# Attention block on one core: value projection by seven block products of 256 columns, position tiles in another order

## The chip, the cores and the metric

One core of a Trainium2 chip runs the whole program. The metric is the device time in microseconds (us), the median of several runs. TensorE (PE; its weight loads are listed as PEld) multiplies, VectorE (DVE), ScalarE (ACT) and GpSimd (POOL) do the element-wise work, SyncE (SP) issues most DMAs.

## The reference, cut to what matters

```python
residual = hidden_states                 # (16, 512, 32, 32), f32
h = group_norm(hidden_states, gamma, beta)
q, k, v = conv1x1(h, wq, bq), conv1x1(h, wk, bk), conv1x1(h, wv, bv)
attn = softmax(einsum('bci,bcj->bij', qf, kf) * C ** -0.5, axis=2)
out = einsum('bcj,bij->bci', vf, attn)
return residual + conv1x1(out, wo, bo)
```

There are 16 images of C = 512 channels and N = 1024 positions.

## The kernel before, in words

**Precision.** A factor of a product is split into a high part (`*_hi`, rounded to the fp32r format) and a low part (`*_lo`, the rest). One `product` (L346 to L349) is three matmuls of 128x128 weights with 512 moving columns: high by high (L347), high by low (L348), low by high (L349). ACT makes the high parts by a copy, DVE the low parts by a subtraction, so that each factor passes ACT and then DVE before PE may use it.

**Weights.** Wk and Wq are multiplied into one matrix before the loop, and so are Wv and Wo. Both joint matrices, split, are kept in DRAM (`kept_t`, `kept_v`), and take turns in the tile `w_split`.

**The stages of PE in an image**, in this order:

1. T (`make_t`): joint Wq/Wk matrix by h. It uses seven block products in place of eight (a Strassen-like scheme), with sums of blocks of h, named S1 to S4, beside the plain blocks A11, A12, A22. 84 matmuls.
2. S (`make_scores`): scores of 1024 x 1024, the same scheme, 168 matmuls. DVE adds up the blocks (`add_s`) and takes the running maximum (`maximum`).
3. V (`make_v`): values, 8 position tiles j of 128 positions x 512 columns, each 4 products of plain blocks (8 block products): 96 matmuls.
4. O0 (`outputs_0`): outputs for the first 512 queries. Outer loop over the 8 position tiles j, inner loop over 4 channel tiles c. 96 matmuls.
5. O1 (`outputs_1`): the other 512 queries. Here c is the outer loop: the first channel tile asks for all 8 position tiles within 24 matmuls. 96 matmuls.

**The softmax** goes beside V, O0 and O1, in two halves of 512 queries. POOL reduces the maximum over partitions (L322, after `maximum`), DVE subtracts it from the scores (`centre`, two tiles a time), ACT takes the exponentials (`exponentials`, two tiles a time), ACT rounds a tile (`high_p`), DVE makes its low part (`low_p`). Then DVE adds the exponentials up (`add_up`), POOL sums over partitions (L333), DVE inverts the sum (`inverse`), and multiplies the outputs by it (`output`). ACT adds a bias, POOL issues an accumulating DMA into `out`.

**The next image** is prepared in O0 and O1: its x is loaded into `room` (`full_in`), ACT normalises it in four pieces (`normalise`), DVE forms S1 to S4 (`sum_h`, four operations), ACT rounds the seven blocks (`high_h`), DVE makes the low parts (`low_h`).

**What sets the order.** There is no scheduler: each engine has one written list of operations, and semaphores hold an operation until what it needs is there. An operation that waits holds everything behind it on its engine. In O1 the wait is this one:

```python
for c in range(KC):
    for j in range(NJ):
        if c == 0:
            pe.wait_ge(p_split, count(b, 16, NJ + j + 1))
```

The first image runs apart (it makes the weights), images 2 to 15 run in a loop, and the last has no next image to prepare (`more` is false).

Of the kernel before, what the change touches and what calls it, by code (L numbers as in the profile page):

```python
# [13 lines left out]
P = 128  # L14
# [22 lines left out]
H_ORDER = (A22, S1, A12, S3, S2, A11, S4)  # L37
H_AT = {x: n + 1 for n, x in enumerate(H_ORDER)}

# [11 lines left out]
G_AT = {PRODUCT_OF[x]: n + 1 for n, x in enumerate(G_ORDER)}  # L51

# [4 lines left out]
def attention_program(nc, x, gamma, beta, wq, bq, wk, wv, bv, wo, bo, out):  # L57
# [17 lines left out]
    TW, VW = 7 * 2 * QUARTER, 3 * 2 * C  # L75
    kept_t = nc.dram_tensor("kept_t", [P, 2, TW], F32).ap()
    kept_v = nc.dram_tensor("kept_v", [P, 2, VW], F32).ap()

    with ExitStack() as ctx:
# [9 lines left out]
        wv_hi, wv_lo = (w_split[:, n, 0:VW].rearrange("p (b k n) -> p b k n", b=3, k=2) for n in range(2))  # L89
# [18 lines left out]
        var_g, rstd, minus_half, primer = sb("var_g", [KC]), sb("rstd", [KC]), sb("minus_half", [KC]), sb("primer", [2])  # L108
        h_scale, h_shift, mean_scaled = sb("h_scale", [KC]), sb("h_shift", [KC]), sb("mean_scaled", [KC])
# [30 lines left out]
        wov_step = scores[:, 14:16, :]  # L140
# [16 lines left out]

        wt_from = {1: b11, 2: b21, 3: b22, 4: neg_d4, 5: d1, 6: d2, 7: d3}
# [3 lines left out]
        v_ring = (6, 7, 4, 5)  # L162
# [11 lines left out]
        full_in = [sem("full_in0"), sem("full_in1")]  # L174
# [29 lines left out]
        o_scaled, o_done = sem("o_scaled"), sem("o_done")  # L204
# [14 lines left out]
        def _(sp):  # L219
# [13 lines left out]
            def image(b, more, first=False):  # L233
# [17 lines left out]
                if first:  # L251

                    sp.wait_ge(t_split, 14)
# [3 lines left out]
                    sp.wait_ge(wvs_split, 3)  # L257
                    for n in range(6):
                        piece(n)
                else:  # L260
                    sp.wait_ge(t_summed, count(b, 14, 14))
                    sp.dma_start(w_split[:, :, 0:VW].bitcast(F32), kept_v).then_inc(wvs_in, 16)
                if more:
# [3 lines left out]
                    if first:  # L267
                        sp.dma_start(kept_v, w_split[:, :, 0:VW].bitcast(F32)).then_inc(kept_v_out, 16)

                    sp.wait_ge(bn_set, count(b, PIECES, 2 * PIECES))  # L270
                    sp.wait_ge(s_added, count(b, 12, 12))
                    for s in range(2):
                        sp.dma_start(full[:, 2 * s:2 * s + 2, :],
                                     x_d[b + 1][:, 2 * s:2 * s + 2, :]).then_inc(full_in[s], 16)
                    sp.wait_ge(v_summed, count(b, 8, 8))
# [69 lines left out]
        def _(pe):  # L345
# [54 lines left out]
            def make_t(b, first=False):  # L400
# [3 lines left out]
                for r in range(2):  # L404
# [3 lines left out]
                    for p in T_ORDER:  # L408
                        if r == 0:
                            pe.wait_ge(h_split, count(b, 7, H_AT[OF_H[p]]))  # L410
# [68 lines left out]

            def make_v(b, first=False):  # L480
                if first:
                    pe.wait_ge(wvs_split, 3)
                else:
                    pe.wait_ge(wvs_in, count(b, 16, 0))
                for j in range(NJ):
                    if j < 2:
                        pe.wait_ge(s_added, count(b, 12, ADD_AT["C21", j]))
                    elif j == 2:
                        pe.wait_ge(c12_copied, count(b, 4, 4))
                    elif j == 3:  # L490
                        pe.wait_ge(s_added, count(b, 12, ADD_AT["C11", 2]))
                    else:
                        pe.wait_ge(v_split, count(b, 8, j - 4 + 1))

                    terms = ((A11, 0), (A12, 1)) if j < KC else ((S1, 0), (A22, 2))
                    for a, w in terms:
                        for k in range(2):
                            mm = product(bank[v_ring[j % 4]][:], h_hi[:, a, k, cols(j % KC)], h_lo[:, a, k, cols(j % KC)],
                                         wv_hi[:, w, k, :], wv_lo[:, w, k, :], w == 0 and k == 0, w > 0 and k == 1)
                    mm.then_inc(v_summed, 1)  # L500

            def outputs_0(b):
                for j in range(NJ):
                    pe.wait_ge(v_split, count(b, 8, j + 1))
                    pe.wait_ge(p_split, count(b, 16, j + 1))
                    for c in range(KC):
                        if j == 0:
                            if c == 0:
                                pe.wait_ge(c12_copied, count(b, 4, 3))
                            else:  # L510
                                pe.wait_ge(s_added, count(b, 12, 12))
                        mm = product(o_bank(c)[:], v_hi[:, j, cols(c)], v_lo[:, j, cols(c)],
                                     p_hi[:, j, :], p_lo[:, j, :], j == 0, j == NJ - 1)
                        if j == NJ - 1:
                            mm.then_inc(o_summed, 1)
                    if j < NJ - 1:
                        mm.then_inc(p_used, 1)

            def outputs_1(b):
                for c in range(KC):  # L520
                    for j in range(NJ):
                        if c == 0:
                            pe.wait_ge(p_split, count(b, 16, NJ + j + 1))
                        mm = product(o_bank(KC + c)[:], v_hi[:, j, cols(c)], v_lo[:, j, cols(c)],
                                     p_hi[:, j, :], p_lo[:, j, :], j == 0, j == NJ - 1)
# [17 lines left out]
        def _(act):  # L543
# [14 lines left out]
            def high_h(b, n, first=False):  # L558
                a = H_ORDER[n]
# [49 lines left out]
            def high_wv(n):  # L609

                act.wait_ge(t_summed, 14)
                act.wait_ge(kept_t_out, 16)
                if n == 2:
                    act.wait_ge(wdv_set, 1)
                else:
                    act.wait_ge(wov_copied, KC)
                nc.scalar.copy(wv_hi[:, n, :, :], wov_step if n == 2 else wov[n]).then_inc(wvs_high, 1)
# [17 lines left out]
            def high_v(b, j):  # L635
                act.wait_ge(v_summed, count(b, 8, j + 1))
                nc.scalar.copy(v_hi[:, j, :], bank[v_ring[j % 4]][:]).then_inc(v_high, 1)  # L637

            def exponentials(b, half, g):
                j = half * NJ + 2 * g  # L640
                act.wait_ge(centred, count(b, 8, half * 4 + g + 1))
# [3 lines left out]
            def high_p(b, half, j):  # L645
                act.wait_ge(exp_set, count(b, 8, half * 4 + j // 2 + 1))
                if half == 1 and j < NJ - 1:
                    act.wait_ge(p_used, count(b, NJ - 1, j + 1))
# [11 lines left out]
            def image(b, more, first=False):  # L660
# [39 lines left out]
                for pair in range(2):  # L700
                    for n, p in enumerate((1, 6, 5)):
                        for q in (2 * pair, 2 * pair + 1):
# [4 lines left out]
                            nc.scalar.copy(snap_s(q, n), bank[alpha_s[q % 2]][:]).then_inc(s_snapped, 1)  # L707
                    for q in (2 * pair, 2 * pair + 1):
# [6 lines left out]
                high_v(b, 0)  # L715
                high_v(b, 1)
                for g in range(4):
                    high_v(b, 2 + g)
                    exponentials(b, 0, g)
                    high_p(b, 0, 2 * g)  # L720
                    high_p(b, 0, 2 * g + 1)
                high_v(b, 6)
                high_v(b, 7)
                for g in range(4):
# [4 lines left out]
                for j in range(3):  # L729
                    high_p(b, 1, j)  # L730
                for j in range(3, NJ):
                    high_p(b, 1, j)
# [435 lines left out]
```

## Time and profile before

| | us |
|---|---|
| median of 3 runs | 2022.17 (2019.12 to 2023.99) |
| profiled execution, its own time | 2020.75 |
| its span, first to last instruction | 2019.0 |
| mean granted TensorE clock | 0.999 |

The page counts PE busy for 99% of the span, DVE and the weight loads for 81%, ACT for 47%, POOL for 16%. Busy shares are averages over stages; in a timeline row the second number is the busy time of the row's instructions, which on DVE and ACT overlap by some 0.1 us where they follow each other, so that the step from one start to the next is the price of one.

### The profile page before, as it was taken

Reading aid. Unit: us, or ns where it says so; the run is one execution under the profiler, and the core shown is the slowest. Engines: PE = TensorE matmul, PEld = TensorE weight load, DVE = VectorE, ACT = ScalarE, POOL = GpSimd, SP = SyncE. Lnnn points to the kernel's source line nnn. Section 1 sums busy time; section 2 is a strip of 40 time slices with the busy share of each in tenths; the row PEclk is TensorE's granted clock in tenths of the full one; section 3 lists DMA queues with packets and bytes.
Section 4 is the critical chain, followed back from the end, with each engine's and each line's share of the span. In section 5 each row is a group of like instructions: output and inputs, shape, how many; then the busy total and the mean of one; then the engine's idle time right before and its main releaser. Section 6 shows DMA issues by size and latency. Waiting matters only on the chain.

```text
span 2019.0 us, 26696 instructions
## 1 busy us (share of the span) xinstructions
PE 1998.6 (99%) x8772; PEld 1645.1 (81%) x8772; DVE 1625.5 (81%) x2120; ACT 956.7 (47%) x1429; POOL 329.8 (16%) x238
## 2 busy tenths in 40 slices
PE   8999999999999999999999999999999999999998
PEld 6888888888888888888888888888888888888887
DVE  8897787978879688796977969788797887969866
ACT  6464442635435463454634536354363543546442
POOL 2021120201202022020121202112020120201202
PEclk9999999999999999999999999999999999999999
DMA  6335252353324435143351523524234342433402
GB/s 240 131 157 147 97 133 105 128 140 156 75 112 140 120 156 118 69 149 111 156 145 69 152 87 150 145 116 113 114 124 136 156 81 105 145 114 156 103 2 42
DMA packets 57033, 247.03 MB, mean 122 GB/s; under 512 B 7728, under 2 KB 7728, under 8 KB 50352
## 3 DMA queue, kind: packets, MB, share of 16 engines
q1 hardware_dynamic: 36464, 213.14, 27.8%
q0 software_dynamic: 18432, 33.56, 11.0%
q10 hardware_dynamic: 2112, 0.01, 0.1%
q8 instruction: 14, 0.23, 0.0%
q14 instruction: 11, 0.09, 0.0%
HBM read 206.32 MB, written 73.92 MB: 139 GB/s over the span
## 4 chain that ended last, share of the span: by engine, by line
PE 89%; DMA 5%; DVE 2%; ACT 1%; issue 1%; POOL 0%; SPq 0%; DVEq 0%; POOLq 0%; ACTq 0%
PE psum L347 30%; PE psum L348 30%; PE psum L349 30%; DMA out<-scores 5%; ACT scores L657 1%; DVE scores L895 0%; DVE wide L1023 0%; DMA scores<-in_wk 0%; DVE bn L756 0%; DVE h_lo L825 0%; POOL out L339 0%; DVE w_split L874 0%; ACT h_hi L564 0%; DVE scores L1029 0%; DVE scores L1015 0%
## 5 line engine op out<-in xcount | busy, mean ns | idle before, releaser
L347 PE MATMUL psum<-big_hi 128*128 128x512 f32 x1056 | 411.5, 390 | 2.8 <-POOL big_lo L297 2.8
L349 PE MATMUL psum<-big_hi,big_lo 128*128 128x512 f32 x1056 | 411.5, 390 | 0.0
L348 PE MATMUL psum<-big_lo,big_hi 128*128 128x512 f32 x1056 | 411.5, 390 | 0.0
L347 PE MATMUL psum<-big_hi,h_hi 128*128 128x512 f32 x896 | 350.1, 391 | 0.8
L349 PE MATMUL psum<-big_hi,h_lo 128*128 128x512 f32 x896 | 348.7, 389 | 0.0
L348 PE MATMUL psum<-big_lo,h_hi 128*128 128x512 f32 x896 | 348.7, 389 | 0.0
L982 DVE TENSOR_TENSOR scores<-psum,room 128x512 f32<-128x512 f32 x192 | 130.8, 689 | 187.3 <-ACT room L707 137.3
L707 ACT COPY room<-psum 128x512 f32<-128x512 f32 x192 | 113.1, 589 | 273.3 <-PE psum L349 273.3
L347 PEld LDWEIGHTS psum<-big_hi 128*128 128x128 f32 x1056 | 198.7, 188 | 44.8 <-DVE big_lo L850 3.0
L349 PEld LDWEIGHTS psum<-big_hi,big_lo 128*128 128x128 f32 x1056 | 198.6, 188 | 41.4
L348 PEld LDWEIGHTS psum<-big_lo,big_hi 128*128 128x128 f32 x1056 | 198.6, 188 | 41.1
L322 POOL PARTITION_ALL_REDUCE wide<-red x32 | 56.9, 1830 | 893.0 <-DVE red L991 893.0
L347 PEld LDWEIGHTS psum<-big_hi,h_hi 128*128 128x128 f32 x896 | 168.2, 188 | 41.1 <-issue 6.6
L347 PE MATMUL psum<-w_split,h_hi 128*128 128x512 f32 x512 | 199.2, 389 | 0.0
L348 PE MATMUL psum<-w_split,h_hi 128*128 128x512 f32 x512 | 199.2, 389 | 0.0
L349 PE MATMUL psum<-w_split,h_lo 128*128 128x512 f32 x512 | 199.2, 389 | 0.0
L349 PEld LDWEIGHTS psum<-big_hi,h_lo 128*128 128x128 f32 x896 | 168.2, 188 | 35.1
L348 PEld LDWEIGHTS psum<-big_lo,h_hi 128*128 128x128 f32 x896 | 168.2, 188 | 34.4
L651 ACT CAST big_hi<-scores 128x512 fp32r<-128x512 f32 x256 | 147.8, 619 | 77.0 <-PE psum L349 74.9
L347 PE MATMUL psum<-h_hi,w_split 128*128 128x512 f32 x448 | 176.1, 393 | 8.1 <-DVE h_lo L825 4.5
L637 ACT CAST big_hi<-psum 128x512 fp32r<-128x512 f32 x128 | 75.4, 589 | 223.4 <-PE psum L349 223.4
L333 POOL PARTITION_ALL_REDUCE wide<-red x32 | 117.7, 3680 | 368.8 <-DVE red L1019 354.9
(117 smaller groups left out, 3274.3 us busy)
## 6 DMA issues: line engine op xcount, KB each, us to landing
w_split<-kept_t SPq DMA_DIRECT2D x15, 3584.0 KB, 11.1
w_split<-kept_v SPq DMA_DIRECT2D x15, 3072.0 KB, 10.6
out<-scores POOLq DMA_DIRECT2D x128, 256.0 KB, 7.4
room<-in_x SPq DMA_DIRECT2D x30, 1024.0 KB, 5.9
room<-in_x SPq DMA_DIRECT2D x60, 256.0 KB, 3.5
red<-in_x SPq DMA_DIRECT2D x30, 256.0 KB, 3.3
wide<-in_x SPq DMA_DIRECT2D x30, 256.0 KB, 7.1
kept_t<-w_split SPq DMA_DIRECT2D x1, 3584.0 KB, 10.9
```

The source lines that it names most:

```text
L322: nc.gpsimd.partition_all_reduce(wide[:, half, :], red[:, half, :], P, MAX_ALL).then_inc(max_all, 1)
L333: nc.gpsimd.partition_all_reduce(wide[:, half, :], red[:, half, :], P, ADD_ALL).then_inc(sum_all, 1)
L347: nc.tensor.matmul(o, a_hi, b_hi, start=start, stop=False, skip_group_check=True)
L348: nc.tensor.matmul(o, a_hi, b_lo, start=False, stop=False, skip_group_check=True)
L349: return nc.tensor.matmul(o, a_lo, b_hi, start=False, stop=stop, skip_group_check=True)
L637: nc.scalar.copy(v_hi[:, j, :], bank[v_ring[j % 4]][:]).then_inc(v_high, 1)
L651: nc.scalar.copy(p_hi[:, j, :], scores[:, half * NJ + j, :]).then_inc(p_high, 1)
L657: nc.scalar.activation(scaled(n), scaled(n), ACT.Identity, bias=out_bias[:, c:c + 1]).then_inc(o_done, 1)
L707: nc.scalar.copy(snap_s(q, n), bank[alpha_s[q % 2]][:]).then_inc(s_snapped, 1)
L982: nc.vector.tensor_tensor(scores[:, o, :], bank[at][:], snap_s(q, n), ALU.add).then_inc(s_added, 1)
```

## The change

It has four parts.

- **V**: 28 products with 256 columns in place of 32 with 512: seven block products p in the order 7, 1, 6, 5, 3, 4, 2, each for the four position quarters q in turn. Each is 2 x 3 matmuls: 168 of 256 columns in place of 96 of 512. ACT copies three partial sums for two pairs of quarters out of PSUM (`snap_v`, 6 operations), DVE adds PSUM to them (`add_v`, 6), and ACT and DVE split the four blocks of each pair (`high_v`, `low_v`, 8 each as before). The joint matrix is kept in seven blocks: `kept_v` grows from 3072 to 3584 KB, and the first image makes seven splits of 512 elements for three of 1024, with four differences of blocks ahead.
- **Order of the position tiles** in O0, O1 and the softmax: 4, 5, 6, 7, 0, 1, 2, 3.
- **The next image**: `room` holds the partial sums of V, so its load comes in four pieces, three of them behind `low_v`. The rounding order of h is A22, A12, A11, S1, S3, S2, S4. DVE does `low_h` of the first three, and the first two `sum_h`, between the seventh and the eighth `low_p` of the second half; the other two `sum_h` come behind it. Before, all four `sum_h` stood ahead of the first `low_p`, and one `low_h` stood ahead of the eighth.
- **The inverse** of the sums, `[128, 512]` with equal partitions: a transpose, a reciprocal of 16 columns and a transpose back.

```diff
-H_ORDER = (A22, S1, A12, S3, S2, A11, S4)
+H_ORDER = (A22, A12, A11, S1, S3, S2, S4)
+V_ORDER = tuple((p, q) for p in (7, 1, 6, 5, 3, 4, 2) for q in range(4))
+J_ORDER = (4, 5, 6, 7, 0, 1, 2, 3)
+G_PAIRS = (2, 3, 0, 1)
...
+            def v_product(q, p):
+                at = (alpha_v if p in (1, 6, 5, 3) else gamma_v)[q // 2] + q % 2
+                for k in range(2):
+                    mm = product(bank[at][:, 0:QUARTER], h_hi[:, OF_H[p], k, cols(q)], h_lo[:, OF_H[p], k, cols(q)],
+                                 wt_hi[:, p - 1, k, :], wt_lo[:, p - 1, k, :],
+                                 k == 0 and p in (7, 1, 2), k == 1 and p in (3, 4, 2))
+                mm.then_inc(v_summed, 1)
...
-                for j in range(NJ):
-                    pe.wait_ge(v_split, count(b, 8, j + 1))
-                    pe.wait_ge(p_split, count(b, 16, j + 1))
+                for n, j in enumerate(J_ORDER):
+                    if n == 0:
+                        pe.wait_ge(v_split, count(b, 8, max(VL_AT["C12", 1], VL_AT["C21", 0], VL_AT["C22", 0])))
...
+                    pe.wait_ge(p_split, count(b, 16, n + 1))
...
-                for g in range(4):
-                    if more:
-                        act.wait_ge(full_in[g // 2], count(b, 16, 16))
-                        normalise(b + 1, g)
-                    exponentials(b, 1, g)
...
+                for n in range(4):
+                    if more and n:
+                        next_full(4 - n)
+                    exponentials(b, 1, n)
+                for n in range(NJ):
+                    high_p(b, 1, n)
+                    if more and n == 2:
+                        next_full(0)
+                    if more and 3 <= n < 6:
...
+                        high_h(b + 1, n - 3)
...
+            def add_v(b, x, r):
+                o = v_snap(v_sums[x], r)
+                dve.wait_ge(v_snapped, count(b, 6, 2 * v_sums[x] + r + 1))
+                dve.wait_ge(v_summed, count(b, 28, V_AT[{"C22": 5, "C21": 4, "C11": 2}[x], 2 * r + 1]))
+                nc.vector.tensor_tensor(o, v_pair(gamma_v[r]), o, ALU.add).then_inc(v_added, 1)
...
-                nc.vector.reciprocal(wide[:, half, :], wide[:, half, :]).then_inc(inv_set, 1)
+                nc.vector.transpose(red[:, half, :], wide[:, half, :]).then_inc(turn_step, 1)
+                nc.vector.reciprocal(column[:], red[:, half, :].rearrange("p (n s) -> p n s", s=BLOCK)[:, :, 0]
+                                     ).then_inc(turn_step, 1)
+                nc.vector.transpose(wide[:, half, :].rearrange("p (n s) -> p n s", s=BLOCK),
+                                    column[:].unsqueeze(2).to_broadcast([P, HALF // BLOCK, BLOCK])).then_inc(inv_set, 1)
...
                 add_up(b, 0)
+                for j in range(4):
+                    low_p(b, 1, j)
+                for n in range(4, NJ - 1):
+                    low_p(b, 1, n)
                 if more:
+                    for n in range(3):
+                        low_h(b + 1, n)
 
                     dve.wait_ge(sum_step, count(b, SUM_STEPS, 3))
-                    for n in range(4):
-                        sum_h(b + 1, n)
-                for j in range(NJ - 1):
-                    low_p(b, 1, j)
+                    sum_h(b + 1, 0)
+                    sum_h(b + 1, 1)
+                low_p(b, 1, NJ - 1)
                 if more:
-                    low_h(b + 1, 0)
-                low_p(b, 1, NJ - 1)
+                    sum_h(b + 1, 2)
+                    sum_h(b + 1, 3)
                 add_up(b, 1)
```

**The order of DVE in O0 and O1, before.** Of an image in the loop. Lines L1015 to L1019 are `add_up`, L810 to L818 `sum_h`, L1002 is `low_p`, L825 `low_h`.

```order
L1019 TENSOR_TENSOR red<-scores 128x512
L810 TENSOR_TENSOR scores<-room 128x1024
L812 TENSOR_TENSOR scores<-room 128x1024
L814 REGISTER_ALU
L815 TENSOR_TENSOR scores<-scores,room 128x1024
L817 REGISTER_ALU
L818 TENSOR_TENSOR scores<-room,scores 128x1024
...
L1002 TENSOR_TENSOR big_lo<-scores,big_hi 128x512
L822 ISA
L825 TENSOR_TENSOR h_lo<-room,h_hi 128x1024
L1002 TENSOR_TENSOR big_lo<-scores,big_hi 128x512
L1015 TENSOR_TENSOR scores<-scores 128x2048
```

**The same place after the change.** L1110 ends `add_up` of the first half, L1082 is `low_p` (seven stand in the gap, the seventh just ahead of L901), L904 is `low_h`, L889 to L897 are `sum_h`, L1106 begins `add_up` of the second half.

```order
L1110 TENSOR_TENSOR red<-scores 128x512
...
L901 ISA
L904 TENSOR_TENSOR h_lo<-room,h_hi 128x1024
L901 REGISTER_ALU
L904 TENSOR_TENSOR h_lo<-room,h_hi 128x1024
L901 REGISTER_ALU
L904 TENSOR_TENSOR h_lo<-room,h_hi 128x1024
L889 TENSOR_TENSOR scores<-room 128x1024
L891 TENSOR_TENSOR scores<-room 128x1024
L1082 TENSOR_TENSOR big_lo<-scores,big_hi 128x512
L893 REGISTER_ALU
L894 TENSOR_TENSOR scores<-scores,room 128x1024
```

Between the seventh and the eighth `low_p` there stood one operation of 1024 elements, and there stand five now.

**The order of ACT after the change**, from the first exponentials of the second half on. L698 is `exponentials`, L599 `normalise`, L708 `high_p`, L608 `high_h`.

```order
L599 ACTIVATE room<-room,h_shift,h_scale 128x1024
L705 REGISTER_ALU
L708 CAST big_hi<-scores 128x512
L814 REGISTER_ALU
L605 ISA
L608 CAST h_hi<-room 128x1024
L705 REGISTER_ALU
L708 CAST big_hi<-scores 128x512
L608 CAST h_hi<-room 128x1024
...
L608 CAST h_hi<-room 128x1024
L708 CAST big_hi<-scores 128x512 x2
```

The last `normalise` moved from ahead of the last exponentials to behind the third `high_p`; the three `high_h` stand behind the fourth, fifth and sixth `high_p`.

## Rows read from the trace of the kernel before

**Rows 1.** The page: busy time, share of the span, instructions of each engine
```profile
PE 1998.6 (99%) x8772; PEld 1645.1 (81%) x8772; DVE 1625.5 (81%) x2120; ACT 956.7 (47%) x1429; POOL 329.8 (16%) x238
```

**Rows 2.** Waits: who waited <- for whom: us in total, times, longest
```profile
PE psum L347 <- DVE h_lo L825: 4.5, 3, 1.6
...
PE psum L347 <- DVE scores L895: 2.8, 5, 0.8
...
PEld psum L347 <- DVE scores L895: 8.4, 12, 1.2
```

**Rows 3.** Windows: stretch, busy us (x) of PE, PEld, DVE, ACT, POOL, PEclk, DMA
```profile
900.10:1000.10 100.00, 100.00 (x442) 82.48 (x441) 77.76 (x109) 49.75 (x77) 12.65 (x9) 1.00 0.42 144
```

**Rows 4.** Timeline of PE, first matmuls of three stages: start us, us, instruction
```profile
714.88 0.39 PE L347 MATMUL psum<-w_split,h_hi 128*128 128x512 f32 x1
...
736.64 0.39 PE L347 MATMUL psum<-big_hi 128*128 128x512 f32 x1
...
780.16 0.39 PE L347 MATMUL psum<-h_hi,w_split 128*128 128x512 f32 x1
```

**Rows 5.** Source line L381: duration ns min/median/max, first and last start
```profile
L381 PEld LDWEIGHTS psum<-ident,scores x16: 139/140/225, 18.6 to 20.3; 128*128 128x128 f32 x16
```

**Rows 6.** Timeline of PE around the longest early wait
```profile
23.42 0.47 PE L347 MATMUL psum<-big_hi 128*128 128x512 f32 x1 [2.78 <-POOL big_lo L297]
```

**Rows 7.** Windows (columns as in rows 3), after that wait
```profile
23.80:27.10 3.30, 3.30 (x10) 2.56 (x9) 3.23 (x5) 1.30 (x2) 3.19 (x3) 0.50 0.02 5
```

**Rows 8.** Timeline of DVE, one image from 719 to 766 us
```profile
721.75 2.97 DVE L996 TENSOR_TENSOR scores<-scores,wide 128x1024 f32<-128x1024 f32 x2
...
738.07 4.62 DVE L996 TENSOR_TENSOR scores<-scores,wide 128x1024 f32<-128x1024 f32 x4
...
742.61 2.28 DVE L1015 TENSOR_TENSOR scores<-scores 128x2048 f32<-128x2048 f32 x1
...
746.19 0.69 DVE L1019 TENSOR_TENSOR red<-scores 128x512 f32<-128x512 f32 x1
...
746.92 1.23 DVE L810 TENSOR_TENSOR scores<-room 128x1024 f32<-128x1024 f32 x1
...
748.06 3.26 DVE L812 TENSOR_TENSOR scores<-room 128x1024 f32<-128x1024 f32 x1
...
753.63 4.29 DVE L1002 TENSOR_TENSOR big_lo<-scores,big_hi 128x512 fp32r<-128x512 f32 x7
...
757.85 1.22 DVE L825 TENSOR_TENSOR h_lo<-room,h_hi 128x1024 fp32r<-128x1024 f32 x1
...
759.32 0.69 DVE L1002 TENSOR_TENSOR big_lo<-scores,big_hi 128x512 fp32r<-128x512 f32 x1 [0.25 <-ACT big_hi L651]
...
764.24 3.35 DVE L1023 RECIPROCAL wide<-wide 128x512 f32<-128x512 f32 x1
```

**Rows 9.** Timeline of ACT, the same image
```profile
739.32 1.06 ACT L642 ACTIVATE scores<-scores 128x1024 f32<-128x1024 f32 x1 [0.75 <-DVE scores L996]
...
741.42 1.04 ACT L642 ACTIVATE scores<-scores 128x1024 f32<-128x1024 f32 x1
...
746.53 2.17 ACT L651 CAST big_hi<-scores 128x512 fp32r<-128x512 f32 x4
...
748.60 1.05 ACT L564 CAST h_hi<-room 128x1024 fp32r<-128x1024 f32 x1
...
759.19 1.05 ACT L564 CAST h_hi<-scores 128x1024 fp32r<-128x1024 f32 x1
...
760.13 1.05 ACT L564 CAST h_hi<-room 128x1024 fp32r<-128x1024 f32 x1
```

**Rows 10.** Timeline of POOL, the same image
```profile
719.69 3.56 POOL L322 PARTITION_ALL_REDUCE wide<-red  x2 [54.78 <-DVE red L991]
...
747.09 4.16 POOL L333 PARTITION_ALL_REDUCE wide<-red  x1 [7.56 <-DVE red L1019]
```

**Rows 11.** The page: groups of instructions | busy us, mean ns of one | idle before
```profile
L982 DVE TENSOR_TENSOR scores<-psum,room 128x512 f32<-128x512 f32 x192 | 130.8, 689 | 187.3 <-ACT room L707 137.3
```

More of the change, by code:

```diff
@@ L251, in image @@
                 if first:
-                    sp.wait_ge(t_split, 14)
+                    sp.wait_ge(wvs_split, 7)
+                    for n in range(6):
+                        piece(n)
                     for c in range(KC):
@@ L707, in image @@
                             nc.scalar.copy(snap_s(q, n), bank[alpha_s[q % 2]][:]).then_inc(s_snapped, 1)
+                            if first and pair == 0 and n < 2:
+                                high_wv(3 + 2 * n + q)
                     for q in (2 * pair, 2 * pair + 1):
@@ L729, in image @@
[L729 to L732, printed above, removed]
-                    if more:
-                        act.wait_ge(v_summed, count(b, 8, 8))
-                        high_h(b + 1, j - 3)
+                snap_v(b, 0, 0)
+                snap_v(b, 0, 1)
+                snap_v(b, 1, 0)
+                snap_v(b, 1, 1)
+                exponentials(b, 0, 0)
+                snap_v(b, 2, 0)
+                exponentials(b, 0, 1)
@@ new lines, in image @@
+                snap_v(b, 2, 1)
+                high_v(b, "C22", 0)
+                high_v(b, "C12", 0)
+                exponentials(b, 0, 2)
+                high_v(b, "C12", 1)
+                high_p(b, 0, 0)
+                high_p(b, 0, 1)
+                high_v(b, "C22", 1)
+                high_v(b, "C21", 0)
+                exponentials(b, 0, 3)
+                high_p(b, 0, 2)
+                high_v(b, "C21", 1)
+                high_p(b, 0, 3)
+                high_v(b, "C11", 0)
@@ new lines, in image, with next_full @@
+                high_p(b, 0, 4)
+                high_v(b, "C11", 1)
+                for n in range(5, NJ):
+                    high_p(b, 0, n)
+                def next_full(k):
+                    act.wait_ge(full_in[k], count(b, 16, 16))
+                    normalise(b + 1, k)
+                for n in range(4):
[7 more added lines that the diff above has]
+                    if more and 3 <= n < 6:
+                        act.wait_ge(v_summed, count(b, 28, 28))
+                        high_h(b + 1, n - 3)
@@ L737, in image @@
                 if more:
-                    high_h(b + 1, 5)
-                    high_h(b + 1, 6)
+                    for n in range(3, 7):
+                        high_h(b + 1, n)
                 if first:
@@ L1131, in image @@
                 if more:
-                    for n in range(1, 7):
+                    for n in range(3, 7):
                         low_h(b + 1, n)
```

233 lines of the change are left out of this document (140 added, 93 removed).

## The prediction

> **What bounds the kernel now.** I read the page first: PE is busy 1998.6 of 2019.0 us [rows 1]. The list of waits says that PE waits for almost nothing: 4.5, 2.8 and (its weight loads) 8.4 us in the whole run [rows 2]. Then the windows: in 100 us in the middle 441 weight loads, one to a matmul, so a matmul of 512 columns takes 100 / 441 = 0.2268 us [rows 3]. 540 of them make 122.4 us an image. The kernel is bound by the number of matmul columns, and a saved matmul is a saved 0.227 us, as long as the other engines still deliver in time. So the second reading is the timeline of one image on DVE, ACT and POOL, where the delivery is seen. Its V stage begins at 714.88, O0 at 736.64, and the next image's T stage at 780.16 [rows 4]. I call 714.88 "V" and count from there: T begins at V+65.3.
>
> **V on PE.** Removed: 96 matmuls of 512 columns, 21.8 us. Added: 168 of 256 columns. No row shows 256 columns. Half of 0.2268 is 0.113; the transposes of 128 columns, each with its own weight load, start their 16 loads from 18.6 to 20.3 us [rows 5], 0.113 apart, so a pair of load and matmul can follow the other about as fast. A load's own duration is longer for the usual operands: busy 82.48 us for 441 in [rows 3], 0.187 each, which is the upper bound, if loads can't overlap. I take 0.120, near the two lower rows: 168 x 0.120 = 20.2 us, 1.6 less an image, 25.6 in all. Bounds: 19.0 and 31.4 us. The Trainium skill (TensorE: Matmul & The Clock Gate, Back-to-back issue gap) lists 262 cycles for 256 columns and 518 for 512, at 2.4 GHz 109 and 216 ns; the row has 227 for the latter. By its figure V would take 18.3 us and save 3.4 us an image.
>
> **What comes in beside it.** DVE gets six `add_v`, like L982: mean 689 ns [rows 11], but in a row seven subtractions of the size take 757.85 - 753.63 = 4.22, 0.603 each [rows 8]. 3.6 us. The two reciprocals cost 3.35 each [rows 8]; two transposes and a short reciprocal I put at 1.7 (two passes like a subtraction and some waits; between 1.4 and 3.35), so DVE's sum is unchanged, but 3.6 us of it come early, in V, and 3.3 us are saved late, behind the point that matters. ACT gets six copies, in V, where it has room. The larger weight load, the four pieces of x, the softmax tiles in another order: nothing, since the load has the whole S stage (38 us) and x is wanted only at V+31. The first image's eight extra short DVE operations lie in its S stage: 0, at most 2 us.
>
> **The moved operations: the chain.** All steps in us after V.
>
> 1. POOL's two reductions of the maximum begin at 719.69 and take 3.56 [rows 10]; the first is ready at 6.6. The first two `centre` were held by them and ended at 721.75 + 2.97 [rows 8]: 9.8. Nothing of this moves.
> 2. DVE then does, up to the first `centre` of the second half: 2 `centre` of 1.135 (4 took 742.61 - 738.07 = 4.54 [rows 8]), 6 `add_v`, 8 `low_v`, 8 `low_p` at 0.603, and the three tiny ones of `affine`, 0.5: 16.0, so 25.8. Walking the two lists of ACT and DVE side by side I find 1.0 of waiting. So that `centre` starts at 26.8 and ends at 28.0. Before it started at 23.2. The other three and `add_up` (742.61 to 746.92 [rows 8], 4.3) keep DVE until 35.6.
> 3. ACT now has no break until the seventh `high_p`: exponentials and `normalise` in pairs of 2.10 (741.42 - 739.32), three of them and one exponentials of 0.97; then `high_p` of 0.52 (4 in 2.07) and `high_h` of 0.94 (760.13 - 759.19) [rows 9]. 28.1 + 6.3 + 1.0 + 3 x 0.52 + 1.13 + 4 x 0.52 + 3 x 0.94 = 43.0. (The first `high_p` ends at 36.0, so from here on DVE waits for ACT. PE releases the seventh tile's place at 20.2 + 7 x 2.72 = 39.3, so that isn't the bound.)
> 4. DVE: `low_p` of the seventh tile, 43.1 to 43.7. Then three `low_h` and two `sum_h` of 1.14 (748.06 - 746.92 [rows 8]): 49.4. Handovers between engines add some 0.3. The eighth `low_p` runs from 49.7 to 50.4. The reduction on POOL that held L812 for 3.26 in place of 1.22 [rows 8, 10] now begins at V+36, where DVE waits for ACT anyway.
> 5. PE: O1 begins at 20.2 + 21.8 = 42.0. The first channel tile takes 3 matmuls, 0.68, a position tile, and asks for the eighth at 46.7. It gets it at 50.4. **PE waits about 3.6 us in every image that has a next one.** Before, the eighth `low_p` ended at 760.0 [rows 8], with PE asking at 758.4 + 4.8 = 763.2: 3.2 us to spare.
>
> So T begins at 65.3 - 1.6 + 3.6 = V+67.3. Since the chain runs from POOL's reduction and not from PE, a faster V doesn't help: the wait grows by as much.
>
> **The clock.** At 23.42 PE had waited 2.78 us [rows 6]. Behind it the granted clock was 0.50, the level of 1.2 GHz, with 10 matmuls touching 3.3 us, where 16 do at 0.227 [rows 7, 3]: 1.4 lost. The new wait is longer than that one. One case doesn't say that it happens each time; I take 10 of 15 images.
>
> **Sum** against the profiled execution's 2020.75 (1.4 below the median): -25.6 for V, +15 x 3.6 = 54 for the wait, +14 for the clock, +2 for the first image: 2065.
>
> **Rivals.**
>
> - **Delivery holds, PE stays the bound.** Then the time is 2020.75 - 25.6 = 1995. (With the 109 ns that the Trainium skill's page TensorE: Matmul & The Clock Gate lists it would be 2020.75 - 54 = 1966, an estimate.) For it: all my steps are sums of rows of another order. Against it: even if ACT and DVE had the seventh tile at once when PE frees its place (39.3), the eighth `low_p` would end at 39.5 + 0.5 + 0.7 + 5.7 + 0.7 = 47.1, 0.4 late: 2001. The turning point is a wait of 1.7 us (25.6 / 15). Chance 0.14.
> - **The chain holds, the clock doesn't fall**: 2050; or it falls each time: 2072. Both are within the forecast's own range.
> - **A later wait comes on top.** The outputs' first half is now scaled later against T (V+58 to 61, T at 67.3), its accumulating DMAs land about 3 us later against the T stage, and DVE's first sum of T waits for them. I find 1 us to spare. If it fails by one or two: 2080 to 2095. Chance 0.09.
> - **Weight loads pace V**: 0.187 x 168 = 31.4 us, 9.6 more an image: 2020.75 + 154 = 2175. Against it stand the loads 0.113 apart [rows 5]. Chance 0.03.
> - **Both effects cancel**: a wait between 1.5 and 2.0 and no fall of the clock, which needs the chain 1.6 us shorter than I find: 2018 to 2025. Chance 0.03.
>
> **How the numbers follow.** A measurement of this kernel can tell 0.2%, 4 us, from no change. The forecast (wait 2.4 to 4.5 us, clock from never to always) has 0.71 and spans 2031 to 2086. Steps 2 and 3 carry its width: without any waiting in step 2 the chain is 1 us shorter, 15 in all. I widen the range to 2025 to 2095, which takes in the later wait and makes 0.8. Faster 0.14, same 0.03, slower 0.83.
>
> **What would show it.** Right: PE's list of waits led by the line of `low_p` (L1082), about 15 times, 3.6 us each, 50 us or more in all; its stretches behind them at clock 0.50; V stages of 20.2 us; O0 free of waits. Wrong: no such wait (then DVE's list was faster than my steps), the wait in another place (`h_lo` or `scores` for T), a V stage of 30 us, or the waits there and no fall of the clock.

## The result, and the profile after

| | before | after |
|---|---|---|
| median of 4 runs, us | 2021.0 (2019.12 to 2023.99) | 2061.35 (2060.27 to 2061.74) |
| profiled execution, its own time | 2020.75 | 2061.74 |
| mean granted TensorE clock | 0.999 | 0.988 |

The ratio is 1.0197, 95% interval 1.018 to 1.0215: the change costs 40 us. The forecast was 2065, in a range of 2025 to 2095.

The page, against [rows 1]: PE is busy for 7 us less, and its share fell from 99% to 97%, since the span is longer.

```profile
PE 1991.7 (97%) x9924; PEld 1694.4 (82%) x9924; DVE 1636.6 (79%) x2287; ACT 999.8 (49%) x1529; POOL 329.3 (16%) x238
```

The values, in the view of groups by form. This is one of three such groups, L382 and L383 are alike.

```profile
L381 PE MATMUL psum<-w_split,h_hi 128*128 128x256 f32 x896 | 253.6, 283 | 0.1
```

The list of waits of PE, against the first two of [rows 2], and of its weight loads, against the third:

```profile
PE psum L381 <- DVE big_lo L1082: 50.5, 15, 3.4
...
PE psum L381 <- DVE h_lo L904: 5.9, 4, 1.8
```

```profile
PEld psum L381 <- DVE big_lo L1082: 56.9, 15, 3.8
...
PEld psum L381 <- DVE scores L974: 0.3, 1, 0.3
```

One wait is new, on L1082, `low_p`: 15 times, once for each image that has a next one. What PE waited for in T is nearly gone: `scores` (L895 before, L974 now) took 8.4 us of the weight loads before, and 0.3 now.

The timeline of PE in one image shows the starts of V, O0 and T, as [rows 4] did, and the matmuls on both sides of the wait:

```profile
856.01 0.28 PE L381 MATMUL psum<-w_split,h_hi 128*128 128x256 f32 x1
...
876.17 0.40 PE L381 MATMUL psum<-big_hi 128*128 128x512 f32 x1
...
902.49 0.39 PE L383 MATMUL psum<-big_hi,big_lo 128*128 128x512 f32 x1
...
906.24 0.67 PE L381 MATMUL psum<-big_hi 128*128 128x512 f32 x1 [3.36 <-DVE big_lo L1082]
...
924.96 0.39 PE L381 MATMUL psum<-h_hi,w_split 128*128 128x512 f32 x1
```

V takes 876.17 - 856.01 = 20.16 us, 168 matmuls of 0.120. O1 starts 96 x 0.2268 = 21.8 later, at 897.9, and asks for the eighth tile 21 matmuls on, at 902.7. The step from 902.49 to 906.24 is 3.75, of which 0.23 is the matmul itself: PE lost 3.52. T begins at V+68.95; before it was V+65.3.

The windows view of the stretch behind the wait (columns as in [rows 3]):

```profile
906.40:909.80 3.40, 3.40 (x9) 2.63 (x10) 3.37 (x3) 2.35 (x3) 0.00 (x0) 0.50 0.00 0
```

The granted clock is 0.50, the level of 1.2 GHz: 9 matmuls touch 3.4 us. It fell so behind the wait in 13 of the 15 images.

The chain on DVE in the same image, to be read against [rows 8]. L1075 is `centre`, L1089 `add_v`, L1082 `low_p`, L904 `low_h`, L889 and L891 the first two `sum_h`, L1117 to L1122 the inverse:

```profile
862.65 4.34 DVE L1075 TENSOR_TENSOR scores<-scores,wide 128x1024 f32<-128x1024 f32 x3 [2.05 <-POOL wide L356]
...
866.91 0.69 DVE L1089 TENSOR_TENSOR room<-psum,room 128x512 f32<-128x512 f32 x1
...
883.01 4.63 DVE L1075 TENSOR_TENSOR scores<-scores,wide 128x1024 f32<-128x1024 f32 x4
...
899.21 0.69 DVE L1082 TENSOR_TENSOR big_lo<-scores,big_hi 128x512 fp32r<-128x512 f32 x1 [0.78 <-ACT big_hi L708]
...
899.82 3.49 DVE L904 TENSOR_TENSOR h_lo<-room,h_hi 128x1024 fp32r<-128x1024 f32 x3
...
903.23 1.22 DVE L889 TENSOR_TENSOR scores<-room 128x1024 f32<-128x1024 f32 x1
...
904.36 1.22 DVE L891 TENSOR_TENSOR scores<-room 128x1024 f32<-128x1024 f32 x1
...
905.50 0.69 DVE L1082 TENSOR_TENSOR big_lo<-scores,big_hi 128x512 fp32r<-128x512 f32 x1
...
912.68 0.70 DVE L1117 STREAM_TRANSPOSE red<-wide 128x512 f32<-128x512 f32 x1
...
913.42 0.25 DVE L1119 RECIPROCAL column<-red 128x16 f32<-128x16 f32 x1
...
913.71 0.71 DVE L1122 STREAM_TRANSPOSE wide<-column 128x512 f32<-128x512 f32 x1
```

And ACT, against [rows 9]: L698 is `exponentials`, L708 `high_p`. The last row is the seventh and eighth tile.

```profile
884.26 1.07 ACT L698 ACTIVATE scores<-scores 128x1024 f32<-128x1024 f32 x1 [4.26 <-DVE scores L1075]
...
891.48 1.64 ACT L708 CAST big_hi<-scores 128x512 fp32r<-128x512 f32 x3
...
898.57 1.13 ACT L708 CAST big_hi<-scores 128x512 fp32r<-128x512 f32 x2
```

Counted from V = 856.02, the first `centre` of the second half starts at 27.0, the seventh tile is rounded from 42.55 on, its low part starts at 43.2, three `low_h` and two `sum_h` run from 43.8 to 49.5, and the eighth low part starts at 49.5.

**Where the 41 us of the profiled execution came from**, by stage, each stage counted from its first matmul to that of the next one:

| stage | before | after | sum of the differences |
|---|---|---|---|
| V, 16 | 21.76 | 20.15, the first 20.54 | -25 |
| O0 and O1, 15 | 43.52 | 48.80 (13 with a falling clock), 47.20 (2) | +76 |
| T, 15 | 19.7 in the mean | 19.04, one 19.42 | -9 |
| S, 16 | 38.21 | 38.08 | -2 |
| first image's T | 24.5 | 26.5 | +2 |

The last line is not the change's: the other kernels below had 24.5 to 24.9 there. In this execution a stretch at the lower clock, from 39.4 to 42.8 us, lay inside that T, which began at 35.8; in the kernel before it lay ahead of T, at 23.8.

### The profile page after: what moved, and what is told of

Read it like the earlier page. It is cut to its first block, busy times and chain, and to the rows that moved or that the text cites. A ratio compares the mean times of both kernels' runs of the same rounds, so it can differ in the third digit from the quotient of the medians.

```text
span 2060.0 us, 29828 instructions
## 1 busy us (share of the span) xinstructions
PE 1991.7 (97%) x9924; PEld 1694.4 (82%) x9924; DVE 1636.6 (79%) x2287; ACT 999.8 (49%) x1529; POOL 329.3 (16%) x238
## 4 chain that ended last, share of the span: by engine, by line
PE 70%; DVE 10%; ACT 8%; issue 7%; DVEq 0%; ACTq 0%; POOL 0%; POOLq 0%
PE psum L381 24%; PE psum L382 23%; PE psum L383 23%; DVE h_lo L904 3%; ACT big_hi L708 2%; DVE big_lo L1082 2%; ACT room L599 2%; DVE big_lo L1098 2%; ACT scores L698 2%; ACT h_hi L608 2%; DVE scores L1075 1%; DVE scores L889 1%; DVE room L1089 1%; DVE red L1070 0%; DVE mean_scaled L880 0%
## 5 line engine op out<-in xcount | busy, mean ns | idle before, releaser
L381 PE MATMUL psum<-big_hi 128*128 128x512 f32 x1056 | 421.5, 399 | 53.6 <-DVE big_lo L1082 50.5
L382 PE MATMUL psum<-big_lo,big_hi 128*128 128x512 f32 x1056 | 419.2, 397 | 0.0
L383 PE MATMUL psum<-big_hi,big_lo 128*128 128x512 f32 x1056 | 418.9, 397 | 0.0
L381 PE MATMUL psum<-big_hi,h_hi 128*128 128x512 f32 x896 | 348.7, 389 | 0.0
L382 PE MATMUL psum<-big_lo,h_hi 128*128 128x512 f32 x896 | 348.6, 389 | 0.0
L383 PE MATMUL psum<-big_hi,h_lo 128*128 128x512 f32 x896 | 348.5, 389 | 0.0
L381 PEld LDWEIGHTS psum<-big_hi 128*128 128x128 f32 x1056 | 203.3, 192 | 102.7 <-DVE big_lo L1082 56.9
L381 PE MATMUL psum<-w_split,h_hi 128*128 128x256 f32 x896 | 253.6, 283 | 0.1
L382 PE MATMUL psum<-w_split,h_hi 128*128 128x256 f32 x896 | 253.6, 283 | 0.0
L383 PE MATMUL psum<-w_split,h_lo 128*128 128x256 f32 x896 | 253.6, 283 | 0.0
L383 PEld LDWEIGHTS psum<-big_hi,big_lo 128*128 128x128 f32 x1056 | 203.1, 192 | 43.5
L382 PEld LDWEIGHTS psum<-big_lo,big_hi 128*128 128x128 f32 x1056 | 203.4, 193 | 41.9
L1082 DVE TENSOR_TENSOR big_lo<-scores,big_hi 128x512 fp32r<-128x512 f32 x256 | 198.7, 813 | 24.9 <-ACT big_hi L708 24.9
L356 POOL PARTITION_ALL_REDUCE wide<-red x32 | 56.9, 1827 | 884.5 <-DVE red L1070 884.5
L381 PEld LDWEIGHTS psum<-big_hi,h_hi 128*128 128x128 f32 x896 | 168.2, 188 | 35.3 <-issue 0.5
L383 PEld LDWEIGHTS psum<-big_hi,h_lo 128*128 128x128 f32 x896 | 168.2, 188 | 34.9
L382 PEld LDWEIGHTS psum<-big_lo,h_hi 128*128 128x128 f32 x896 | 168.2, 188 | 34.8
L1075 DVE TENSOR_TENSOR scores<-scores,wide 128x1024 f32<-128x1024 f32 x128 | 162.9, 1324 | 32.7 <-POOL wide L356 32.7
L381 PE MATMUL psum<-h_hi,w_split 128*128 128x512 f32 x448 | 175.5, 392 | 5.9 <-DVE h_lo L904 5.9
L367 POOL PARTITION_ALL_REDUCE wide<-red x32 | 104.1, 3252 | 478.5 <-DVE red L1110 469.5
```

The source lines that it names most:

```text
L356: nc.gpsimd.partition_all_reduce(wide[:, half, :], red[:, half, :], P, MAX_ALL).then_inc(max_all, 1)
L367: nc.gpsimd.partition_all_reduce(wide[:, half, :], red[:, half, :], P, ADD_ALL).then_inc(sum_all, 1)
L381: nc.tensor.matmul(o, a_hi, b_hi, start=start, stop=False, skip_group_check=True)
L382: nc.tensor.matmul(o, a_hi, b_lo, start=False, stop=False, skip_group_check=True)
L383: return nc.tensor.matmul(o, a_lo, b_hi, start=False, stop=stop, skip_group_check=True)
L1075: nc.vector.tensor_tensor(scores[:, j:j + 2, :], scores[:, j:j + 2, :], wide[:, half, :].unsqueeze(1).to_broadcast([P, 2, HALF]), ALU.subt ...
```

## The experiments

All are compared with the changed kernel's 2061.35, and each set ran beside the kernel before, whose medians were 2018.7 to 2021.2.

### The order between the seventh and the eighth tile

```diff
-                for n in range(4, NJ - 1):
+                for n in range(4, NJ):
                     low_p(b, 1, n)
                 if more:
                     for n in range(3):
                         low_h(b + 1, n)
...
                     sum_h(b + 1, 0)
                     sum_h(b + 1, 1)
-                low_p(b, 1, NJ - 1)
```

> The changed kernel with one line moved: DVE makes the low part of the eighth softmax tile directly behind the seventh, ahead of the three low_h and two sum_h. Theory (chain and order): the tile is ready at V+44.6 where PE asks at V+46.7, so the 3.5 us wait in O1 goes in all 15 images and the clock no longer falls there (13 falls). DVE's list is not shorter, so its last output multiplication stays near V+69.9, now T+6 in place of T+1, and the DMAs behind it hold up the T stage by 0 to 3 us: 2061 - 53 - 23 + 1.5 x 15 = 2008, between 1985 and 2030. Rival (V's extra DVE and ACT work alone makes the tile late, whatever stands between): the wait stays, 2061.

Measured: 2031.66 (2031.16 to 2034.55), ratio to before 1.0067 (1.005 to 1.0083). The O stages last 43.55 us each, the wait and the falls of the clock in them are gone (76 us), but the T stages last 22.1 in place of 19.1 (46 us). I had 1.5 us a T for the middle, with 3 as the upper end; it was 3, so the time is just above my upper end of 2030. PE's waits and two rows of DVE's timeline of one T stage show it:

```profile
PE psum L381 <- DVE scores L974: 19.1, 19, 2.0
...
PE psum L381 <- ACT scores L669: 8.9, 15, 0.8
```

```profile
1288.54 0.75 DVE L974 SCALAR_TENSOR_TENSOR scores<-psum,t_step,scores 128x512 f32<-128x512 f32 x1 [1.51 <-DMA out<-scores]
...
1299.15 0.75 DVE L974 SCALAR_TENSOR_TENSOR scores<-psum,t_step,scores 128x512 f32<-128x512 f32 x1 [4.10 <-DMA out<-scores]
```

The second value of each DVE row is the busy time, the bracket says how long DVE stood idle and for what: for the DMAs that store the outputs of the image before. The list of DVE has that wait in front of D3, in each half of T.

In one of the 15 T stages the clock fell as well, behind a wait of only 2.0 us:

```profile
1050.71 0.50 PE L381 MATMUL psum<-h_hi,w_split 128*128 128x512 f32 x1 [1.97 <-DVE scores L974]
```

```profile
1051.60:1055.00 3.40, 3.40 (x10) 2.62 (x9) 3.37 (x7) 0.86 (x3) 0.00 (x0) 0.50 0.00 0
```

Only the two sums moved, the three `low_h` left in their place:

```diff
+                low_p(b, 1, NJ - 1)
+                if more:
                     dve.wait_ge(sum_step, count(b, SUM_STEPS, 3))
                     sum_h(b + 1, 0)
                     sum_h(b + 1, 1)
-                low_p(b, 1, NJ - 1)
-                if more:
                     sum_h(b + 1, 2)
```

> The changed kernel with only the two sum_h moved behind the eighth low_p; the three low_h stay between the seventh and it. Theory (the wait in O1 is the sum of what stands between, less the slack): the wait is 3.53 - 2 x 1.14 = 1.25 us in 15 images. Such a wait doesn't make the clock fall: O stages last 44.9. T then starts 3.8 us earlier against DVE's tail and waits some 1.5 us: 2061.35 - 34 - 23 + 22 = 2026, between 2012 and 2036. Rival (ACT or another engine holds the tile too): the wait stays above 2 us.

Measured: 2033.1 (2030.31 to 2035.31). PE's waits:

```profile
PE psum L381 <- DVE big_lo L1082: 16.6, 15, 1.2
...
PE psum L381 <- DVE scores L974: 14.0, 18, 1.4
```

In the trace the steps of PE at this place are 1.48 us, so 1.25 are lost, exactly 3.52 less two operations of 1.14. The clock stayed at its upper level in every image, and O stages lasted 44.95. T stages lasted 20.6 (23 us more in sum). So the wait is what stands between the two tiles, less the slack, and nothing else holds the tile.

### The order alone, in the kernel before

```diff
-H_ORDER = (A22, S1, A12, S3, S2, A11, S4)
+H_ORDER = (A22, A12, A11, S1, S3, S2, S4)
...
                 add_up(b, 0)
-                if more:
...
-                    dve.wait_ge(sum_step, count(b, SUM_STEPS, 3))
-                    for n in range(4):
-                        sum_h(b + 1, n)
                 for j in range(NJ - 1):
                     low_p(b, 1, j)
                 if more:
-                    low_h(b + 1, 0)
+                    for n in range(3):
+                        low_h(b + 1, n)
...
+                    dve.wait_ge(sum_step, count(b, SUM_STEPS, 3))
+                    sum_h(b + 1, 0)
+                    sum_h(b + 1, 1)
                 low_p(b, 1, NJ - 1)
+                if more:
+                    sum_h(b + 1, 2)
+                    sum_h(b + 1, 3)
...
```

> The kernel before with nothing but the new order of the next image's preparation (rounding order of h; three low_h and two sum_h between the seventh and eighth low_p, two behind). Theory: without the heavier V the eighth tile comes at V+48.7 where PE asks at V+48.3, so O1 waits only 0.4 us and the clock stays; but DVE idles while it waits for ACT, where it made the sums before, its tail is 4 us later and T waits about 2 us: 2021 + 15 x 2.4 = 2057, between 2025 and 2065. Rival 1 (order alone makes the change's loss in O1): 3.5 us waits in O1 with a falling clock, 2097. Rival 2 (order is free without V): 2021.

Measured: 2057.47 (2057.07 to 2060.21), ratio 1.0195 (1.0178 to 1.0212). O stages last 44.15 (0.6 more), T stages 21.5 (1.8 more), and the clock never falls, not even behind a wait of 2.8 us in T.

```profile
PE psum L350 <- DVE scores L898: 21.3, 14, 2.8
...
PE psum L350 <- DVE big_lo L1005: 4.4, 15, 0.3
```

The same order that costs 3.5 us a wait with the new V costs 0.6 with the old one. So the order alone doesn't make the wait of 3.5 us, and neither does the new V when nothing stands between the two tiles (e1). The new V with the old order of the next image's preparation was not run. But the order is a loss by itself, of another sort: it makes DVE late for T. That the total comes out near the changed kernel's is a coincidence of two different sums.

### The clock

```diff
+                        if c == 0 and n == NJ - 1 and more:
+                            for _ in range(15):
+                                nc.tensor.matmul(bank[7][:], v_hi[:, J_ORDER[0], 0:P], p_hi[:, J_ORDER[0], :],
+                                                 start=True, stop=True, skip_group_check=True)
                         if c == 0:
```

> The changed kernel with 15 matmuls of 512 columns into a free PSUM bank ahead of PE's wait in O1 (images 1 to 15), whose results nothing reads. Theory: they fill the wait (15 x 0.227 = 3.4 us), the granted clock stays at its upper level, the wait's own 53 us stay: 2061 - 23 = 2038. Rival (the slower matmuls behind the wait are hidden or belong to the wait itself): 2061; more than 2061 if the fillers delay PE beyond the tile's arrival.

Measured: 2043.12 (2041.77 to 2043.78), mean clock 0.999. All 15 O stages last 47.2 us, as the two images of the changed kernel whose clock had not fallen. PE's longest entry is now one of the first image:

```profile
PE psum L381 <- DVE h_lo L908: 5.9, 4, 1.7
```

18 us less: 21 in the O stages (13 falls of 1.6 us each), less 3 that came back in T. So the falls of the clock took 21 us of the changed kernel's O stages, and 18 of its time, in a kernel that computes the same. I had forecast 2038; what came back in T is most of the difference.

### The inverse

```diff
-                nc.vector.transpose(red[:, half, :], wide[:, half, :]).then_inc(turn_step, 1)
...
+                nc.vector.reciprocal(wide[:, half, :], wide[:, half, :]).then_inc(inv_set, 1)
```

> The changed kernel with the inverse undone: the reciprocal of 512 columns for transpose, short reciprocal, transpose. Theory: both stand behind the eighth low_p, so the wait in O1 stays 3.5 us; DVE's tail comes 3.3 us later, T+4 in place of T+1, where before had T+2.8: 2061 to 2071. Rival (DVE's total work sets the period): 15 x 3.3 = 50 more, 2111.

Measured: 2081.5 (2079.35 to 2083.12), 20 more than the changed kernel: a miss, since my upper end was 10 more, and less than half of the rival's 50. The wait in O1 is the same, and T has waits again:

```profile
PE psum L381 <- DVE big_lo L1082: 50.4, 15, 3.4
...
PE psum L381 <- DVE scores L974: 7.6, 13, 1.4
```

T stages last 20.0 (15 us more in sum), and the O stages 7 more: the clock fell in 14 images, and the stretch at the lower clock lasted 6.8 us in five of them, where the changed kernel had only 3.4. So the shorter inverse is a good part of the change; DVE's tail had less slack against T than I gave it.

### What the late tail costs, and where

In T, DVE waits for the stored outputs of the second half before D3, though D3 and D1 write rows 5 and 4, and the outputs lie in rows 0 to 3:

```diff
-                if not first:
-                    for n in range(KC, 2 * KC):
-                        dve.wait_ge(out_stored[n], count(b, 16, 0))
                 add_t(b, 1, "D3")
...
                 add_t(b, 1, "D1")
+                if not first:
+                    for n in range(KC, 2 * KC):
+                        dve.wait_ge(out_stored[n], count(b, 16, 0))
                 add_t(b, 1, "D2")
```

This was put into three kernels. Into e1's:

> e1 (eighth low_p first), and in the T stage DVE waits for the stored outputs of the second half ahead of D2, the first sum that overwrites their rows, in place of D3. Theory (e1's 3.0 us a T stage are DMA landings that DVE's first sum waits for, late because DVE's tail is late against an earlier T): the larger of the two waits in T, 1.2 to 1.8 us each, goes: 2031.7 - 15 x 1.6 = 2008, between 2000 and 2014; the 0.7 to 1 us at the start of T stays. Rival (T waits for DVE's own lateness, the DMA is only the last to come): no more than 5 us gained, 2027.

Measured: 2005.1 (2004.83 to 2005.4), ratio to before 0.9923 (0.9907 to 0.994). T stages last 20.4 on average.

```profile
PE psum L381 <- ACT scores L669: 9.1, 15, 0.8
...
PE psum L381 <- DVE scores L974: 2.4, 4, 0.9
```

What is left is mostly ACT, whose first snapshot of T waits until all of h is split.

Into the kernel before:

> The kernel before with the same wait moved from D3 to D2. Its T stages last 19.7 us where 84 matmuls make 19.04, so at most 0.66 x 15 = 10 us can be had: 2018.75 - 10 = 2009, between 2007 and 2013. Rival: its gaps are of another kind, 2019.

Measured: 2009.14 (2008.83 to 2009.91), ratio 0.9943 (0.9927 to 0.996). All its T stages but the first image's last 19.04. The kernel before took 2020.55 beside it, so this wait was 11 us of it: 10 in T, and the rest in S, whose stages shrank from 38.21 to 38.08.

Into the changed kernel:

> The changed kernel with the wait for stored outputs moved from D3 to D2, which was worth 10 us in the kernel before and 27 in e1. Theory: here T begins so late that it has no waits (19.04 us a stage), so nothing is gained: 2061, within 3. Rival: 10 us gained, 2051.

Measured: 2060.94 (2060.17 to 2061.34). The same edit is worth 27, 11 or 0 us, depending on whether the wait in O1 has already given T its slack.

### Is the chain free of PE?

My prediction said that the tile's time hangs on POOL's reduction and not on PE. So work added to PE in V should cost nothing:

```diff
                         pe.wait_ge(s_added, count(b, 12, ADD_AT["C21", q]))
+                        if q == 1:
+                            for _ in range(8):
+                                nc.tensor.matmul(bank[7][:], h_hi[:, A22, 0, 0:P], h_hi[:, A22, 0, :],
+                                                 start=True, stop=True, skip_group_check=True)
```

> The changed kernel with work added: 8 matmuls of 512 columns at the start of V (1.8 us of PE in each image) into a bank that the next product overwrites. Theory (the eighth tile comes by the chain from POOL's reduction, whatever PE does): the wait in O1 shrinks by 1.8 to 1.7 us, a wait of that size doesn't make the clock fall, the images last as long or shorter: 2061.35 - 23 for the clock + 2 for the last image = 2040, between 2036 and 2063. Rival (V's length is on the path): 29 us more, 2090.

Measured: 2086.32 (2082.39 to 2089.35). A miss: the rival's 2090. The wait in O1 stayed 3.5 us in each of the 15 images, and the V stages are 29 us longer in sum. The O stages are 7 us shorter, since the clock fell in only 8 images behind the same wait; why in fewer is open. The row of DVE's first `add_v` tells why the wait stayed:

```profile
875.85 0.69 DVE L1093 TENSOR_TENSOR room<-psum,room 128x512 f32<-128x512 f32 x1 [1.76 <-ACT room L688]
```

It waits 1.76 us for ACT's copy of the third partial sum (L688), which waits for PE's product 5. In the changed kernel the same operation starts at 866.91 without a wait, V+10.9; ACT's copy, 0.58 from 866.29, ended at 866.87. The two arrive together, with no slack at all. Up to product 5 the chain does run through PE. Behind that point it should not:

```diff
                     pe.wait_ge(p_split, count(b, 16, n + 1))
+                    if n == 0:
+                        for _ in range(8):
+                            nc.tensor.matmul(bank[3][:], v_hi[:, j, 0:P], p_hi[:, j, :],
+                                             start=True, stop=True, skip_group_check=True)
                     for c in range(KC):
```

> As e9, but the 8 added matmuls (1.8 us) stand at the start of O0, behind everything of V that DVE's first sums wait for. e9 showed DVE waiting 1.76 us at its first add_v, so its chain hangs on PE's V up to product 5. Theory, mended: behind that point PE's length doesn't touch the chain: the wait in O1 is 3.53 - 1.8 = 1.7 us, too short for the clock to fall: 2061 - 23 + 2 = 2040, between 2036 and 2046. Rival (PE's length is on the path everywhere): 2086 as e9.

Measured: 2045.04 (2044.21 to 2046.46), **16 us less than the changed kernel, with 29 us of PE work added**, and 41 less than the same work 20 us earlier in the image.

```profile
PE psum L381 <- DVE big_lo L1086: 23.3, 15, 1.6
```

The waits are 1.7 us each, and no clock falls behind them.

### A version that beats both

It keeps the new V, the short inverse and the order of the tiles, and changes three things at once: DVE's list behind the tiles of the second half, the rounding order to fit it, and the rows of T's temporaries, so that the waits for stored outputs stand at D2 in both halves and ACT's first snapshot need not wait for h.

```diff
-H_ORDER = (A22, A12, A11, S1, S3, S2, S4)
+H_ORDER = (A22, S1, S3, A12, S2, A11, S4)
...
-        snap_t = {"a": 6, "b": 7, "y": 14}
-        sum_t = [{"D3": 8, "D1": 9, "D2": 10, "B11": 11, "B22": 12, "B21": 13},
+        snap_t = {"a": 15, "b": 7, "y": 14}
+        sum_t = [{"D3": 12, "D1": 13, "D2": 8, "B11": 9, "B22": 10, "B21": 11},
                  {"D3": 5, "D1": 4, "D2": 0, "B11": 1, "B22": 2, "B21": 3}]
...
+            snap_t["b"] = 7 if first else 5
+            sum_t[1]["D3"], sum_t[1]["D1"] = (5, 4) if first else (7, 6)
...
+                for n in range(4, NJ):
+                    low_p(b, 1, n)
+                if more:
+                    dve.wait_ge(sum_step, count(b, SUM_STEPS, 3))
+                    sum_h(b + 1, 0)
+                    sum_h(b + 1, 1)
+                add_up(b, 1)
+                inverse(b, 0)
...
+                for n in range(KC):
+                    output(b, n)
+                if more:
+                    sum_h(b + 1, 2)
+                    sum_h(b + 1, 3)
+                    for n in range(3):
+                        low_h(b + 1, n)
...
+                inverse(b, 1)
+                for n in range(KC, 2 * KC - 1):
+                    output(b, n)
+                if more:
+                    low_h(b + 1, 3)
+                    low_h(b + 1, 4)
+                output(b, 2 * KC - 1)
+                if more:
+                    low_h(b + 1, 5)
+                    low_h(b + 1, 6)
```

> A version that should beat both: the changed kernel's V, with the eighth low_p directly behind the seventh; two sum_h, add_up, the inverse and the first four outputs next, S2 and S4 later; rounding order of h A22, S1, S3, A12, S2, A11, S4, with the low parts of the last four around the last output; in T the rows of the snapshots and sums chosen so that D3 and D1 touch no row that a DMA still reads, and the waits for the stored outputs at D2 of each half. Theory: no wait in O1, at most a few tenths in T, clock at its upper level: 2061.35 - 53 - 23 = 1985, up to 1995. Rival (the work on DVE is too much for a shorter image, whatever the order): 2005 or more, with waits in T.

Measured: **1983.81 (1983.6 to 1985.35), ratio to before 0.982 (0.9803 to 0.9836)**. These are all of PE's waits, and all lie in the first image, the last (0.2 us) in its V:

```profile
PE psum L385 <- DVE h_lo L908: 4.8, 3, 1.7
...
PE psum L385 <- POOL big_lo L335: 2.8, 1, 2.8
...
PE psum L395 <- DVE h_hi L911: 1.6, 1, 1.6
...
PE psum L385 <- ACT room L688: 0.2, 1, 0.2
```

Every T but the first image's lasts 19.04 us, every S 38.08, every V but the first 20.15, every O0 with O1 43.55. With V's 25 us, T's 10 and S's 2 taken off the kernel before, its 2020 gives 1983: nothing of the gain is lost any more. The fair measure of V is e6, the kernel before without its waits in T: 2009.14, 25 us more than this one. Of the 37 us against the kernel before, 11 are not the change's but the moved wait's. The three things were not measured one by one on the way from e5's 2005.1.

## Why the prediction was right, point by point

- **What bounds the kernel**: right. PE's matmul columns; and e8 against e6 (25 us) shows that V's saving is had in full once the deliveries are in time.
- **V on PE**, 0.120 us a matmul of 256 columns: right, 20.16 us a stage. The Trainium skill (TensorE: Matmul & The Clock Gate, Back-to-back issue gap) lists 262 cycles for 256 columns, 109 ns at 2.4 GHz, and calls it the gap of isolated matmuls. It is not met here: the trace has 120 ns, beside a weight load for each matmul.
- **DVE's and ACT's new work**: the inverse takes 912.68 to 914.56, 1.9 us with its waits (1.7 forecast).
- **The chain, steps 1 to 5**: right to 0.2 us up to the wait. `centre` at V+27.0 (26.8), the seventh low part at 43.2 (43.1), the eighth from 49.5 to 50.2 (49.7 to 50.4), a wait of 3.52 (3.6). e7 and e1 took it apart as the steps say.
- **"Since the chain runs from POOL's reduction and not from PE, a faster V doesn't help"**: the half of this that was tested, in e9, is wrong. Steps 1 and 2 walk the lists of ACT and DVE, and have no term for when PE's partial sums are there. PE up to product 5 and POOL's reduction arrive at DVE together, so a slower V costs its full length (29 us in e9's V stages). It was right behind that point (e11). A faster V wasn't tried; that the reduction would then be the later one is argued, not shown.
- **The clock**: right in kind. It fell 13 times for 10 taken, and cost 1.6 us for 1.4: 21 us for 14. How often it falls was a guess, and stays one: behind the same wait it fell in 13, 13, 14 and 8 of 15 images (changed kernel, e10, e3, e9).
- **The sum**: 2065 for 2061, in part because errors cancel. The clock is 7 short. On the other side a term was missing, the waits of 0.7 us a T stage that the kernel before had and that a later T would end: 9 us. I named T's waits in [rows 2] and gave the change nothing for them. The S stages gave another 2 us. The profile's first image was 2 us longer, as allowed for, but that is luck: I had allowed for extra operations on DVE, and what came was a stretch at the lower clock inside its T. The terms that carry the forecast, V (25 for 25.6) and the waits (15 x 3.52 = 53 for 54), were right by themselves.
- **The rivals**: the later wait in T didn't come, but e3 shows that it was near: 3.3 us on DVE's tail bring 1 us a T. Weight loads didn't pace V.

## What to carry to other kernels

On an engine with one fixed list, find the operation that another engine asks for at a known time, and add up what stands ahead of it, for the new list and the old one; here five preparations for the next image ahead of one 0.7 us subtraction turned a saving of 25 us into a loss of 40, and the same operations behind it, with the temporaries' rows sorted out, kept all 25. Slack is not additive: the same edit was worth 27, 11 or 0 us, so a wait that shows nothing in a profile can be what holds back the next improvement. A short stall of PE costs more than its length when the clock falls behind it.

## What the runs showed of the hardware

- Matmuls of 256 columns in fp32r, each with its own load of 128x128 weights, start 0.120 us apart at the upper clock, those of 512 columns 0.227. If the time is a fixed part and one in proportion to the columns, the fixed part is about 0.013, an estimate from these two.
- Behind waits of 3.52 us the clock fell in 13 of 15 images (14 in e3, 8 in e9), behind waits of 1.25 (e7) and 1.7 us (e11) in none of 15. The length of a wait doesn't decide alone: in T it fell behind one of 2.0 us in e1, and not behind one of 2.8 us in e4. In e3 the stretch at the lower level lasted twice as long in five images.
- Fifteen matmuls that nobody reads, put into a wait, made the kernel 18 us faster (e2), and eight in a place where PE had time 16 us (e11), by keeping the clock up.
- A transpose of 128x512 f32 on DVE takes 0.70 us, and two of them with a reciprocal of 16 columns 1.9, where the reciprocal of 512 columns takes 3.35.
